# Depthwise convolution as fp32 products on 32x32 tiles of TensorE, pointwise product on 32x128 tiles

## The chip, the cores and the metric

The kernel runs on one core of a Trainium2 chip. The metric is the device time of one execution in microseconds; the profile's span, from the first to the last instruction, lies within a few tenths of a per cent of it. The core has five engines with queues of their own: TensorE (PE in the profile, its weight loads PEld), VectorE (DVE), ScalarE (ACT), GpSimd (POOL) and SyncE (SP), which issues DMAs. They work side by side and wait for each other through semaphores.

## What is computed

The input is 16 images of 128 channels and 28x28 points in fp32. A block of depthwise and pointwise convolution is added to it, then an attention over the 784 points of each image as tokens, then a mixture of eight experts. The change touches only the first block:

```python
h = conv(gn(x), dw_w, padding=1, feature_group_count=128)   # 3x3, one filter per channel
h = h + dw_b
h = relu(bn(h, bn1))
h = prune(h, 4.0)        # a channel whose maximum over the image is below 4.0 becomes zero
h = conv(h, pw_w)        # 1x1, 128 -> 128
h = h + pw_b
h = relu(bn(h, bn2))
h = prune(h, 0.001)
x = x + h
```

`gn` is a group norm over groups of four channels. After it come the spiking attention with a causal mask (queries, keys and values are projected and compared with thresholds) and the experts with their router.

## The kernel before

Each engine has its own instruction stream, written by hand, and the order in it is the order of the code. The image loop has 20 steps. Step k holds five stages at once, for different images: group norm of image k (`norm`), convolution of k-1 (`cnv`), transposes, layer norm and projections of k-2 (`add`), scores and attention of k-3 (`att`), the router and the sending of rows of k-4 (`moe`). Steps 0 to 5 and 14 to 19 are written out, the others run in a hardware loop, two steps a turn. After the loop come 105 tiles of 256 rows for the experts, and a last part that sums and writes the images.

The convolution of an image is a product per tap. Input and taps are split in two fp16 parts each: ScalarE writes the normalised image times 64 to `xn64` (L731) and its fp16 rounding to `padx[:, 0]` (L735), and GpSimd writes the rest to `padx[:, 1]` (L416). `make_taps` (L934, L937) puts the 9 taps of each channel on diagonals of 128x128, high and low part. `conv` (L475) then makes, for 9 taps and two halves of the image, three products (high-high, high-low, low-high) of 128x128 with 392 columns, 54 in all, which add up in PSUM `pair_a`. TensorE's `body` cuts these 54 into six pieces, `conv(..., first, end)` with 3 products to a unit: one unit after the scores 0 to 2, one after score 3, one after score 4, three after the transposes of `x1` and `t2`, eight after the attention, and four after the transposes of `xn`. Then come `queries`, `values`, `keys`, and last `pointwise`.

ScalarE's `first_relu` turns `pair_a` into `h1` (L742). VectorE's `mask_weights` takes the maximum of each channel (L1016), compares it with 4.0 (L1017) and scales the rows of the pointwise weights by the result (L1018, `pw_masked`). `pointwise` (L485) is two fp32 products of 392 columns. ScalarE's `second_relu` (L749) makes `h2`, and VectorE's `add_block` adds it to `x1`. On VectorE `mask_weights` stands between the spikes of the queries (`sq`) and those of the values (`sv`) and keys (`sk`), all L1032.

GpSimd does, in each step, the subtraction L416, the subtraction of the router's rows (L423) and 14 indirect DMAs (L428).

Engines' names for the four PSUM pairs of two banks are `pair_a` to `pair_d`; the convolution and the pointwise product both use `pair_a`.

## Time and profile before

| | us |
|---|---|
| median of 3 runs | 928.25 |
| lowest, highest | 926.79, 929.76 |
| profiled execution, its span | 927.2 |
| TensorE busy in it | 740.9 (80%) |
| VectorE busy | 687.4 (74%) |
| GpSimd busy | 525.4 (57%) |
| ScalarE busy | 480.0 (52%) |

The rows are read so: times are in us from the start of the span unless marked ns; `x` stands ahead of a number of records; L475 is a line of the kernel; in the names of tiles buffer numbers are left out, so that `h<-pair_a` is `h1` or `h2`, and `xn` in L731 is `xn64`. An fp32 product with a 128x128 stationary side shows as two records. A record of TensorE ends some time after the next one has started, since products are pipelined.

### The profile page before, as it was taken

Reading aid. Unit: us, or ns where it says so; the run is one execution under the profiler, and the core shown is the slowest. Engines: PE = TensorE matmul, PEld = TensorE weight load, DVE = VectorE, ACT = ScalarE, POOL = GpSimd, SP = SyncE. Lnnn points to the kernel's source line nnn. Section 1 sums busy time; section 2 is a strip of 40 time slices with the busy share of each in tenths; the row PEclk is TensorE's granted clock in tenths of the full one; section 3 lists DMA queues with packets and bytes.
Section 4 is the critical chain, followed back from the end, with each engine's and each line's share of the span. In section 5 each row is a group of like instructions: output and inputs, shape, how many; then the busy total and the mean of one; then the engine's idle time right before and its main releaser. Section 6 shows DMA issues by size and latency. Waiting matters only on the chain.

```text
span 927.2 us, 24122 instructions
## 1 busy us (share of the span) xinstructions
PE 740.9 (80%) x6865; PEld 578.0 (62%) x6866; DVE 687.4 (74%) x2275; ACT 480.0 (52%) x1102; POOL 525.4 (57%) x498
## 2 busy tenths in 40 slices
PE   1599989999999998996403999999999999994433
PEld 0255656666666665664302988889888988894322
DVE  2656887888888887865751898989888898884444
ACT  1235655566666664654302767777667766672000
POOL 4100176677777666665772576777677777765000
PEclk9989998999999998996555999999999999998555
DMA  7102132232323231221142232323222322222998
GB/s 151 58 18 76 53 111 89 83 106 81 105 83 107 79 107 42 66 71 48 61 85 53 68 89 72 86 82 83 80 80 76 85 84 83 75 79 54 269 286 234
DMA packets 76644, 85.72 MB, mean 92 GB/s; under 512 B 12491, under 2 KB 60655, under 8 KB 76610
## 3 DMA queue, kind: packets, MB, share of 16 engines
q1 hardware_dynamic: 59698, 52.85, 22.2%
q0 software_dynamic: 13888, 26.03, 8.9%
q10 hardware_dynamic: 3024, 6.43, 1.9%
q8 instruction: 17, 0.28, 0.1%
q14 instruction: 17, 0.14, 0.0%
HBM read 44.27 MB, written 35.48 MB: 86 GB/s over the span
## 4 chain that ended last, share of the span: by engine, by line
PE 65%; DVE 10%; DMA 8%; POOL 6%; issue 5%; ACT 4%; SPq 1%; POOLq 0%; DVEq 0%; ACTq 0%
PE pair_d L673 16%; PE pair_a L475 14%; PE pair_b L657 8%; PE pair_c L657 7%; DMA w<-expert_rows 6%; POOL dispatched_rows L428 4%; PE pair_c L506 3%; PE pair_a L645 3%; ACT seen_g L772 2%; PE pair_d L571 2%; PE pair_b L495 2%; PE pair_d L544 2%; PE pair_c L557 2%; PE pair_b L501 1%; DVE pw_masked L1018 1%
## 5 line engine op out<-in xcount | busy, mean ns | idle before, releaser
L438 POOL DMA_INDIRECT expert_rows<-xb_x,dest x210 | 243.0, 1157 | 114.3 <-issue 74.9
L428 POOL DMA_INDIRECT dispatched_rows<-rows,pos x224 | 217.5, 971 | 98.8 <-issue 63.8
L673 PE MATMUL pair_d<-w,xb_x 128*128 x2520 | 172.5, 220 | 0.0
L475 PE MATMUL pair_a<-padx,tap_diag 128*128 128x392 f16 x864 | 167.2, 341 | 0.9 <-ACT h L749 0.9
L673 PEld LDWEIGHTS pair_d<-w,xb_x 128*128 128x128 f16 x2520 | 153.0, 98 | 6.4
L1201 DVE TENSOR_TENSOR xb_x<-seen_g,xb_x 128x512 f16<-128x512 f32 x210 | 134.9, 681 | 0.0
L475 PEld LDWEIGHTS pair_a<-padx,tap_diag 128*128 128x128 f16 x864 | 84.5, 101 | 59.7 <-issue 6.0
L826 ACT ACTIVATE xrt<-pair_a 128x512 f16<-128x512 f16 x105 | 62.6, 597 | 113.4 <-PE pair_a L645 113.4
L1198 DVE CAST xb_x<-seen_g 128x512 f16<-128x512 f32 x210 | 89.9, 468 | 6.7 <-ACT seen_g L837 6.7
L837 ACT ACTIVATE seen_g<-pair_b,b 128x256 f32<-128x256 f32 x212 | 83.2, 475 | 6.2 <-PE pair_b L657 3.5
L837 ACT ACTIVATE seen_g<-pair_c,b 128x256 f32<-128x256 f32 x208 | 81.7, 475 | 5.4 <-PE pair_c L657 2.2
L657 PE MATMUL pair_b<-xrt,w 128*128 128x256 f16 x636 | 79.6, 276 | 1.8 <-ACT xrt L826 1.8
L657 PE MATMUL pair_c<-xrt,w 128*128 128x256 f16 x624 | 77.9, 275 | 1.9 <-ACT xrt L826 1.9
L645 PE MATMUL pair_a<-ident,xr 128*128 128x128 f16 x420 | 41.4, 223 | 45.0 <-DMA xr<-dispatched_rows 34.7
L416 POOL TENSOR_TENSOR padx<-xn,padx 128x784 f16<-128x784 f32 x16 | 26.2, 1637 | 89.9 <-ACT padx L735 89.7
L1187 DVE TENSOR_SCALAR small<-xr,tile_expert 128x2 f32<-128x2 f32 x105 | 27.6, 263 | 53.2 <-DMA expert_rows<-xb_x,dest 31.6
L657 PEld LDWEIGHTS pair_b<-xrt,w 128*128 x636 | 59.0, 98 | 11.6 <-issue 2.3
L657 PEld LDWEIGHTS pair_c<-xrt,w 128*128 x624 | 59.4, 99 | 8.5 <-issue 2.2
L789 ACT ACTIVATE root<-var 128x15 f32<-128x15 f32 x20 | 4.3, 214 | 107.1 <-DVE var L997 107.1
L645 PEld LDWEIGHTS pair_a<-ident,xr 128*128 128x128 f16 x420 | 27.6, 99 | 49.4 <-DMA xr<-dispatched_rows 34.8
L754 ACT ACTIVATE xn<-pair_b,shift,rstd 112x128 f32<-112x128 f32 x112 | 40.9, 466 | 20.6 <-DVE shift L1007 20.6
L506 PE MATMUL pair_c<-xt,w_t 128*128 128x272 f32 (+1 forms) x128 | 49.1, 507 | 1.1 <-ACT xt L762 1.1
(184 smaller groups left out, 1290.3 us busy)
## 6 DMA issues: line engine op xcount, KB each, us to landing
xr<-dispatched_rows SPq DMA_DIRECT2D x105, 131.0 KB
xb_x<-in_x SPq DMA_DIRECT2D x32, 392.0 KB, 3.8
w<-expert_rows SPq DMA_DIRECT2D x16, 784.0 KB, 7.1
t_all<-t SPq DMA_DIRECT2D x16, 392.0 KB
out<-w ACTq DMA_DIRECT2D x16, 392.0 KB, 6.4
w_stage<-in_L_ffn_W SPq DMA_DIRECT2D x16, 256.0 KB, 4.4
dispatched_rows<-rows,pos POOLq DMA_INDIRECT x224, 2.3
expert_rows<-xb_x,dest POOLq DMA_INDIRECT x210
```

The lines of the kernel that those rows point to most:

```text
L428: pool.indirect_dma_start(xs, bass.IndirectOffsetOnAxis(ap=pos[:, u, t, k:k + 1].bitcast(U32), axis=0), rows[:, u, t, :].bitcast(U32), Non ...
L438: pool.indirect_dma_start(ys, bass.IndirectOffsetOnAxis(ap=dest[:, u, s:s + 1].bitcast(U32), axis=0), y[:, u, s, :], None, bounds_check=ta ...
L475: last = T.matmul(pa[:, h * BANK:h * BANK + HALF], tap_diag[:, wp, tap, :], padx[:, xp, u, ky + 14 * h:ky + 14 * h + 14, kx:kx + SIDE], st ...
L506: last = T.matmul(pc[:, c0:c1], w_t[:, w, :], xt[:, c0:c1], start=True, stop=True)
L645: last = T.transpose(turned[:, c0:c0 + P], xr[:, u, s, part * P:(part + 1) * P], ident16[:])
L657: last = T.matmul(hp[:, f * TILE:(f + 1) * TILE], w1[:, wp, bass.ds(w0 + f * P, P)], xrt[:, u % 2, 2 * xp:2 * xp + 2, :].rearrange("p s k ...
L673: last = T.matmul(dst, ghl[:, u % 2, gp, f * TILE + s * P:f * TILE + (s + 1) * P], w2[:, wp, bass.ds(w0 + f * P, P)], start=False, stop=(f ...
L754: last = A.activation(out_[:, t, :], pair[0:TT, t * P:(t + 1) * P], ACT.Identity, scale=rstd[0:TT, n0 + t:n0 + t + 1], bias=shift[0:TT, n0 ...
L826: A.activation(xrt[:, u % 2, :, :].rearrange("p s k -> p (s k)"), turned[:, 2 * BANK * (u % 2):2 * BANK * (u % 2) + 4 * P], ACT.Copy).then ...
L837: A.activation(g[:, u % 2, f, :], hp[:, f * TILE:(f + 1) * TILE], ACT.Gelu, scale=1.0 / WSCALE, bias=b1[:, bass.ds(c0 + f, 1)]).then_inc(S ...
L1198: V.tensor_copy(ghl[:, u % 2, 0, h * 2 * TILE:(h + 1) * 2 * TILE], gv(u, h)).then_inc(S["g_hi_ready"], 1)
L1201: V.tensor_tensor(ghl[:, u % 2, 1, h * 2 * TILE:(h + 1) * 2 * TILE], gv(u, h), ghl[:, u % 2, 0, h * 2 * TILE:(h + 1) * 2 * TILE], ALU.subt ...
```

## The change

The input is no longer split. `padx` is fp32 and ScalarE writes it in one pass from `xb` (`xn64`, L731 and GpSimd's L416 are gone). The taps are no longer split either: `tap_diag` holds nine tables of 32 columns, made by one product in the set-up.

`conv` cuts the channels in four groups of 32 (`c`) and the image in four quarters of 7 rows (`q`). A product takes the 32 channels of `c` and writes the quarter `q` to the 32 partitions `q`, with 196 columns, on the 32x32 tile of rows `c` and columns `q`. A unit of the order in `body` is now one tap for two channel groups, eight products. The first nine units are the channel groups 0 and 1, the last nine 2 and 3; in between TensorE waits for its own products (`conv_half`), since groups 0 and 2, and 1 and 3, share a PSUM bank. The units stand where they stood. After it a partition holds channel 32c + r of quarter q at 32q + r.

So `first_relu` is four instructions, one for each channel group, with constants spread by TensorE in the set-up (`bn_q`). The maximum of a channel now lies in four partitions. `find_live` takes the maximum in each and compares it, `fold_live` adds the four comparisons up by a product on TensorE, and `mask_weights` compares the sum with 0.5 and scales a table of 128x512, the pointwise weights spread over the four quarters (`pw_q`). `pointwise` is 16 fp32 products of 196 columns on 32x128 tiles, in two halves with a wait of TensorE for itself in between. `gate` is a wait that stands as an instruction of its own.

```diff
-                for p in range(first, end):
-                    tap, h = p // 2, p % 2
+                for n in range(first, end):
+                    half, tap = n // TAPS, n % TAPS
+                    if n == TAPS:
+                        gate("conv_half", i + 1)
                     ky, kx = tap // 3, tap % 3
-                    for m, (wp, xp) in enumerate(((0, 0), (0, 1), (1, 0))):
-                        last = T.matmul(pa[:, h * BANK:h * BANK + HALF], tap_diag[:, wp, tap, :],
-                                        padx[:, xp, u, ky + 14 * h:ky + 14 * h + 14, kx:kx + SIDE],
-                                        start=(tap == 0 and m == 0), stop=(tap == TAPS - 1 and m == 2))
+                    for c in (2 * half, 2 * half + 1):
+                        for q in range(Q):
+                            last = T.matmul(pa[q * B:(q + 1) * B, quarter_at(c):quarter_at(c) + QL], tap_diag[c * B:(c + 1) * B, tap, :],
+                                            padx[c * B:(c + 1) * B, u, ky + QROWS * q:ky + QROWS * q + QROWS, kx:kx + SIDE],
+                                            start=(tap == 0), stop=(tap == TAPS - 1), tile_position=(c * B, q * B))
+                    if n == TAPS - 1:
+                        last.then_inc(S["conv_half"], 1)
                 if end == 2 * TAPS:
                     last.then_inc(S["conv_ready"], 1)
 
+            def fold_live(i):
+
+                pe.wait_ge(S["live_ready"], i + 1)
+                T.matmul(pa[:, QL:QL + Q], same[:, :, :].rearrange("p q b -> p (q b)"), live[:, 1, :], start=True, stop=True).then_inc(S["live_folded"], 1)
+
             def pointwise(i):
-                pe.wait_ge(S["pwm_ready"], i + 1)
-                pe.wait_ge(S["h1_ready"], i + 1)
-                for h in range(2):
-                    last = T.matmul(pa[:, h * BANK:h * BANK + HALF], pw_masked[:], h1[:, h * HALF:(h + 1) * HALF], start=True, stop=True)
+                gate("pwm_ready", i + 1)
+                for half in range(2):
+                    if half == 1:
+                        last.then_inc(S["pw_half"], 1)
+                        gate("pw_half", i + 1)
+                    for c in range(Q):
+                        for q in (2 * half, 2 * half + 1):
+                            last = T.matmul(pa[:, quarter_at(q):quarter_at(q) + QL], pw_masked[q * B:(q + 1) * B, c, :], h1[q * B:(q + 1) * B, c, :],
+                                            start=(c == 0), stop=(c == Q - 1), tile_position=(q * B, 0))
                 last.then_inc(S["pw_ready"], 1)
...
-                A.activation(xn64[:, :], xb[:, u, :], ACT.Identity, scale=gs[:, 22:23], bias=shift[:, GN:GN + 1]).then_inc(S["xn_ready"], 1)
                 if some(i - 1):
                     act.wait_ge(S["conv_ready"], i - 1)
-                act.wait_ge(S["xn_ready"], i + 1)
-                A.activation(padx[:, 0, u, 1:1 + SIDE, 1:1 + SIDE], xn64[:, :].rearrange("p (h w) -> p h w", w=SIDE),
-                             ACT.Identity).then_inc(S["xhi_ready"], 1)
+                A.activation(padx[:, u, 1:1 + SIDE, 1:1 + SIDE], xb[:, u, :].rearrange("p (h w) -> p h w", w=SIDE),
+                             ACT.Identity, scale=rstd[:, GN:GN + 1], bias=shift[:, GN:GN + 1]).then_inc(S["xn_ready"], 1)
...
-                A.activation(h1[:, :].rearrange("p (h c) -> p h c", h=2), halves(pa), ACT.Relu,
-                             scale=bn[:, 0, 2:3], bias=bn[:, 0, 7:8]).then_inc(S["h1_ready"], 1)
+                for c in range(Q):
+                    last = A.activation(h1[:, c, :], pa[:, quarter_at(c):quarter_at(c) + QL], ACT.Relu, scale=bn_q[:, 0, c:c + 1], bias=bn_q[:, 1, c:c + 1])
+                last.then_inc(S["h1_ready"], 1)
...
+            V.tensor_tensor(tap_diag[:, :, :], bc_mid(fold[:, :], TAPS), bc_last(dw_w[:, :], B), ALU.mult).then_inc(S["taps_ready"], 1)
...
-            def mask_weights(i):
+            def find_live(i):
 
                 link = Chain("dve_x", DVE_STEPS["x"] * i)
                 dve.wait_ge(S["h1_ready"], i + 1)
+                link(V.tensor_reduce(live[:, 0, :], h1[:, :, :], AX.X, ALU.max))
+                V.tensor_scalar(live[:, 1, :], live[:, 0, :], DW_THRESH, None, ALU.is_ge).then_inc(S["live_ready"], 1)
+
+            def mask_weights(i):
+
+                link = Chain("dve_x", DVE_STEPS["x"] * i + 1)
+                dve.wait_ge(S["live_folded"], i + 1)
                 if some(i):
                     dve.wait_ge(S["pw_ready"], i)
-                link(V.tensor_reduce(gs[:, 24:25], h1[:, :], AX.X, ALU.max))
-                link(V.tensor_scalar(gs[:, 25:26], gs[:, 24:25], DW_THRESH, None, ALU.is_ge))
-                V.tensor_scalar(pw_masked[:], w_t[:, 3, :], gs[:, 25:26], None, ALU.mult).then_inc(S["pwm_ready"], 1)
+                link(V.tensor_scalar(live[:, 2, :], pa[:, QL:QL + Q], 0.5, None, ALU.is_ge))
+                V.tensor_tensor(pw_masked[:, :, :], pw_q[:, :, :], bc_last(live[:, 2, :], P), ALU.mult).then_inc(S["pwm_ready"], 1)
```

On TensorE the end of a step, from the attention to the pointwise product, read before:

```order
L557 MATMUL pair_c<-seen_g,sv 128x112
L475 MATMUL pair_a<-padx,tap_diag 128x392 x24
L501 MATMUL pair_b<-ident,xn 128x112 [waits xn1_ready]
L501 MATMUL pair_b<-ident,xn 128x112 x6
L475 MATMUL pair_a<-padx,tap_diag 128x392 x12
L506 MATMUL pair_c<-xt,w_t 128x512 [waits xt_ready,gvar_ready,t2_ready]
L506 MATMUL pair_c<-xt,w_t 128x272
L525 MATMUL pair_b<-w_t,xt 112x128 x7
L506 MATMUL pair_c<-xt,w_t 128x512 [waits sq_ready]
L506 MATMUL pair_c<-xt,w_t 128x272
L485 MATMUL pair_a<-h,pw_masked 128x392 [waits h1_ready,pwm_ready]
L485 MATMUL pair_a<-h,pw_masked 128x392
```

and reads now:

```order
L497 MATMUL pair_a<-padx,tap_diag 32x196 x24
L497 MATMUL pair_a<-padx,tap_diag 32x196 [waits conv_half]
L497 MATMUL pair_a<-padx,tap_diag 32x196 x39
L535 MATMUL pair_b<-ident,xn 128x112 [waits xn1_ready]
L535 MATMUL pair_b<-ident,xn 128x112 x6
L497 MATMUL pair_a<-padx,tap_diag 32x196 x32
L540 MATMUL pair_c<-xt,w_t 128x512 [waits xt_ready,gvar_ready,t2_ready]
L540 MATMUL pair_c<-xt,w_t 128x272
L559 MATMUL pair_b<-w_t,xt 112x128 x7
L508 MATMUL pair_a<-live,same 128x4 [waits live_ready]
L540 MATMUL pair_c<-xt,w_t 128x512 [waits sq_ready]
L540 MATMUL pair_c<-xt,w_t 128x272
```

24 products have become 64 and 12 have become 32; the wait for `conv_half` falls into the piece after the attention, and the product with `live` and its wait stand between the values and the keys. Behind the keys now stand 8 products, a wait for `pw_half` and 8 more.

On VectorE the same end of a step read before:

```order
L1032 TENSOR_SCALAR sq<-pair_c 128x784 [waits q_ready,dve_z]
L1016 TENSOR_REDUCE gs<-h 128x1 [waits pw_ready,h1_ready]
L891 ISA
L1017 TENSOR_SCALAR gs<-gs 128x1 [waits dve_x]
L891 REGISTER_ALU
L1018 TENSOR_SCALAR pw_masked<-w_t,gs 128x128 [waits dve_x]
L1032 TENSOR_SCALAR sv<-pair_b 112x896 [waits v_ready]
L1032 TENSOR_SCALAR sk<-pair_c 128x784 [waits k_ready]
```

and reads now:

```order
L1067 TENSOR_SCALAR sq<-pair_c 128x784 [waits q_ready,dve_z]
L1043 TENSOR_REDUCE live<-h 128x4 [waits h1_ready]
L922 ISA
L1044 TENSOR_SCALAR live<-live 128x4 [waits dve_x]
L1067 TENSOR_SCALAR sv<-pair_b 112x896 [waits v_ready]
L1052 TENSOR_SCALAR live<-pair_a 128x4 [waits pw_ready,live_folded]
L922 REGISTER_ALU
L1053 TENSOR_TENSOR pw_masked<-pw_q,live 128x512 [waits dve_x]
L1067 TENSOR_SCALAR sk<-pair_c 128x784 [waits k_ready]
```

The making of `pw_masked` has moved behind `sv`, and has grown from 128 to 512 elements in each partition.

## Rows read from the trace of the kernel before

**Rows 1.** The page's busy times; then one step by engine (busy us, records, granted clock).

```profile
PE 740.9 (80%) x6865; PEld 578.0 (62%) x6866; DVE 687.4 (74%) x2275; ACT 480.0 (52%) x1102; POOL 525.4 (57%) x498
...
307.53:331.07 23.54, 22.41 (x147) 14.96 (x146) 19.96 (x77) 14.19 (x28) 17.29 (x17) 1.00 0.37 109
```

**Rows 2.** Timeline of that step, first part: start, length, engine, line, names, records.

```profile
312.59 0.26 ACT L772 ACTIVATE seen_g<-pair_d 112x112 bf16<-112x112 f32 x1
...
312.75 0.97 PE L495 MATMUL pair_b<-ident,xb_x 128*112 128x128 f32 x7 [0.28 <-ACT seen_g L772]
...
318.50 4.22 PE L475 MATMUL pair_a<-padx,tap_diag 128*128 128x392 f16 x24
...
319.93 2.56 ACT L754 ACTIVATE xn<-pair_b,shift,rstd 112x128 f32<-112x128 f32 x7 [1.28 <-DVE shift L1007]
...
322.56 0.87 PE L501 MATMUL pair_b<-ident,xn 112*128 112x112 f32 x7
```

**Rows 3.** Waits of TensorE: who waited for whom, total us, times, longest.

```profile
PE pair_a L485 <- DVE pw_masked L1018: 9.1, 3, 3.4
PE pair_b L501 <- ACT xn L754: 6.4, 2, 5.3
```

**Rows 4.** Timeline of that step, last part: TensorE, ScalarE, VectorE.

```profile
323.27 2.23 PE L475 MATMUL pair_a<-padx,tap_diag 128*128 128x392 f16 x12
...
325.33 1.48 PE L506 MATMUL pair_c<-xt,w_t 128*128 128x512 f32 x4
...
325.59 1.00 ACT L742 ACTIVATE h<-pair_a,bn 128x784 f32<-128x784 f32 x1 [0.51 <-PE pair_a L475]
...
326.65 1.69 PE L525 MATMUL pair_b<-w_t,xt 128*112 128x128 f32 x14
...
327.81 0.96 DVE L1016 TENSOR_REDUCE gs<-h 128x1 f32<-128x784 f32 x1
...
328.18 1.48 PE L506 MATMUL pair_c<-xt,w_t 128*128 128x512 f32 x4
...
328.81 0.15 DVE L1017 TENSOR_SCALAR gs<-gs 128x1 f32<-128x1 f32 x1
...
329.65 1.58 PE L485 MATMUL pair_a<-h,pw_masked 128*128 128x392 f32 x4
...
331.07 0.19 PE L579 MATMUL pair_d<-chosen,before 112*128 112x64 bf16 x1
```

**Rows 5.** Small products: timeline twice, then the group by line (busy us, mean ns).

```profile
314.33 1.45 PE L571 MATMUL pair_d<-wr_c,t 128*112 128x8 f32 x14
315.63 1.69 PE L475 MATMUL pair_a<-padx,tap_diag 128*128 128x392 f16 x9
...
331.10 0.32 PE L582 MATMUL pair_d<-chosen,ones 112*128 112x56 bf16 x7
...
L582 PE MATMUL pair_d<-chosen,ones 112*128 112x8 bf16 x16 | 2.7, 166 | 0.0
```

**Rows 6.** Timeline of the first step: the taps and the first convolution.

```profile
24.53 1.85 DVE L934 TENSOR_SCALAR tap_diag<-ident,dw 128x128 f16<-128x128 f32 x9
...
26.42 3.81 DVE L937 SCALAR_TENSOR_TENSOR tap_diag<-ident,dw,tap_diag 128x128 f16<-128x128 f32 x9
...
32.32 11.66 PE L475 MATMUL pair_a<-padx,tap_diag 128*128 128x392 f16 x54
```

**Rows 7.** Chain of work, its two longest L1018; then timelines of VectorE and GpSimd.

```profile
134.79 3.64 DVE pw_masked L1018
...
352.60 4.07 DVE pw_masked L1018
...
319.81 0.97 DVE L1046 TENSOR_TENSOR t<-pair_c,xb_x 128x784 f32<-128x784 f32 x1
...
353.15 1.64 POOL L416 TENSOR_TENSOR padx<-xn,padx 128x784 f16<-128x784 f32 x1
354.72 1.84 POOL L423 TENSOR_TENSOR rows<-xf,rows 112x896 f16<-112x896 f32 x1
```

96 lines of the change are left out of this document (56 added, 40 removed).

## The prediction, written before the changed kernel ran

> **What bounds the kernel now.** I read the page's table of engines first, then the stretches of one step of the image loop, then the waits of TensorE, then the timeline of that step. TensorE is busy 80% of the span, more than any other [rows 1]. The change touches the image loop only: the part up to about 430 us, in which 20 steps run and 16 of them hold a convolution. In the step from 307.53 to 331.07 TensorE is busy 22.41 of 23.54 us at the full granted clock (1.00), VectorE 19.96, GpSimd 17.29, ScalarE 14.19 [rows 1]. So at first sight every microsecond taken from TensorE's work is won. The timeline corrects that. The step holds four stretches, and in three of them TensorE's convolution pieces only fill a wait for someone else:
>
> - Scores: ScalarE's seven sign passes, of which the last starts at 312.59, set the pace, and the first transpose of the next piece starts at 312.75, released by them after a wait of 0.28 us [rows 2]. The first 9 of the 54 convolution records stand inside this.
> - From there to the transposes of `xn` at 322.56 runs a chain: the transposes at 312.75, statistics on VectorE (behind logits that don't depend on the convolution), scales, seven normalisations of 2.56 us from 319.93, which end at 322.49 [rows 2]. 33 convolution records stand in this stretch; they end just as the chain does. The waits view has TensorE waiting 6.4 us in two steps for this `xn` already [rows 3].
> - The last 12 records run from 323.27 to the projection at 325.33 [rows 4].
> - From 325.33 on TensorE alone decides: projections, then the pointwise product at 329.65, which was kept waiting by VectorE's `pw_masked` [rows 4].
>
> A faster convolution therefore finds the end of a chain in the first three stretches, and a slower tail costs in full.
>
> **The convolution itself.** Before: 54 records of 392 columns; 24 of them take from 318.50 to 322.56, 169 ns each, so 9.1 us per image [rows 2]. After: 144 products on 32x32 tiles with 196 columns, in fp32. An fp32 product is two records: two products of 512 and 272 columns show as x4, and take 325.33 to 326.65, which is 1.32 us for 2 x 784 columns, 0.84 ns a column and record [rows 4]. So 288 records of 196 x 0.84 = 165 ns each, 47.5 us if nothing overlaps. No row of this trace shows two tiles at work at once, so the cost is bounded from both sides. Low: eight tiles at a time, 16 records stream in 2 x 165 = 0.33 us, 18 such groups make 5.9 us. High: 47.5 us. Between them stand two floors that rows do show. Pairs of load and product with 8 to 56 columns start (0.32 - 0.17) / 6 = 25 ns apart [rows 5], which gives 288 x 25 = 7.2 us. With 8 columns and fp32 weights 14 records take from 314.33 to 315.63, 93 ns each for 112 weight columns, 0.83 ns a weight column [rows 5]; 32 columns are 27 ns and 288 loads 7.8 us. I take 7.8 us, because these two rows are the nearest to small tiles: one has many short products, the other small fp32 ones. The eight tiles of a group have places of their own in the array, and the two channel groups write to different banks, so nothing in the code orders them. To this comes one wait of TensorE for itself between the halves: a record of 8 columns lasts 0.166 us [rows 5], so the end of a product comes that long after its columns, and with a semaphore and a load I put it at 0.35 us. Sum 8.2 us in place of 9.1. The 0.9 us that this saves lie almost wholly in the first three stretches and are **costed at nothing**: the sign passes and the `xn` chain are late next. If that cover were gone they would be worth 16 x 0.9 = 14 us. In the third stretch 64 records of 27 ns take 1.7 us in place of 2.0, and ScalarE reaches the copy of `xt` one instruction sooner, since `padx` is written in one pass: **-0.3 us** a step.
>
> **The tail.** Three things grow here, all on the path.
> - ScalarE writes `h1` in four pieces. 128 columns take 2.56 / 7 = 0.37 us, 784 take 1.00 [rows 2, 4]; 196 columns come to 0.43, four to 1.7 in place of 1.0. `h1` is then ready at 325.59 + 1.7 = 327.3, and VectorE, busy with `sq` until then, takes it up at 327.81 [rows 4]: hidden by 0.5 us.
> - VectorE finds the live channels (reduction 0.96, comparison 0.15) by 328.96 [rows 4]. The new wait on TensorE stands behind `values` and ahead of `keys`. TensorE could have gone on at 328.18 and goes on at about 329.05; queued behind it are the keys, the pointwise product, the ranks and the next scores. The fold costs two loads, 0.2 us. VectorE then does `sv`, the second comparison (0.15) and the product of 128x512. 784 elements take 0.97 and 1 takes 0.15 [rows 4, 7], 1.05 ns each, so the 896 of `sv` take 1.08, until 329.98, and 512 take 0.69. That is 330.87, and the pointwise product starts at 330.95 in place of 329.65: **+1.3 us**.
> - The pointwise product is 16 products of 196 columns on 32x128 tiles, 32 records in place of 4, two row groups at a time: 32 x 165 / 2 = 2.6 us if two really stream together, 32 x 107 = 3.4 us if the loads of 128 fp32 weight columns (128 x 0.83) go one by one. I take 3.0, and 0.35 for the wait between its halves, in place of 1.42 (329.65 to 331.07) [rows 4]: **+1.9 us**.
>
> Net 1.3 + 1.9 - 0.3 = +2.9 us a step, x 16 = **+46.4 us**.
>
> **What goes for good.** In the first step the tap matrices take VectorE from 24.53 to 30.15, and the first convolution starts at 32.32 behind the statistics that come after them [rows 6]. The new table is one product of 128x288 in the set-up, where VectorE waits for ScalarE anyway; the longer set-up there (two reductions, three small products, five copies) is put at 2 us and lies ahead of the first scales, which wait for ScalarE, so it is costed at nothing; without that cover it costs its 2 us, once. The first convolution then starts near 26.7: **-5.6 us**. The subtraction L416 leaves GpSimd. Twice the 128x128 scaling L1018 took 3.64 and 4.07 us in place of 0.29 (L1016 and L1017 give 1.05 ns an element beside 0.15), and the second time it ends when GpSimd's L416 and L423 end, back to back (353.15 to 356.56) [rows 7]; TensorE waited for it 9.1 us in all, three times [rows 3]. With L416 gone only L423 is left to collide with, and I count 3.4 + 3.7 = **-7.1 us**. The Trainium skill (SBUF — State Buffer, SBUF: two separate sides) says that VectorE and GpSimd share a port pair; by it the new product, which reads two tables in SBUF, could still wait up to 1.8 us for L423, and 16 such waits would add 29 us, which I leave to the range.
>
> **Sum.** 46.4 - 5.6 - 7.1 = +33.7 us on the profiled 927.2 us; the median lies 1.05 us above the profiled span, so **962 us**. Ends of the forecast case, by step: tail +0.9, pointwise +1.5 and third stretch -0.9 give 1.5 x 16 - 12.7 = +11, 940 us; tail +1.6, pointwise +2.3, nothing in the third stretch and an allowance of 1 us for going in and out of the tiles, which no row shows, give 4.9 x 16 = +78, less 8 if GpSimd's L423 takes some of the gain back, = +70, 998 us.
>
> **Rivals.**
> 1. Records of one tile hold up the stream. The two records of one product stand next to each other on the same tile. If records start strictly in their order, the second waits until the first has streamed, and all behind it wait too; only the second record of one tile and the first of the next run together. Each product then costs 165 ns, 144 of them 23.8 us. For it: in every row of this trace starts follow the program. Against it: no row has two tiles. A step grows by 23.8 - 9.1 = 14.7, less 1.0 of TensorE's idle time that it fills (23.54 - 22.41), plus 3.2 in the tail: 16.9 x 16 - 12.7 = +258, **1186 us**. The Trainium skill (TensorE: Matmul & The Clock Gate, Part 3: Packing small matmuls — row/col tiling) says that products start and end strictly in program order; it also reports 10.6 times the speed for 16 tiles with one product each, which supports the forecast. No run here shows either yet.
> 2. No overlap at all: 47.5 us a convolution, 40.6 x 16 - 12.7: **1565 us**.
> 3. The granted clock falls. It is 1.00 in the step shown [rows 1]. If work on small tiles lets it drop to the lower level, 1.2 GHz, in the loop, the rest of TensorE's step, 22.41 - 9.1 - 1.4 = 11.9 us, doubles, the convolution becomes 18 x 0.66 = 11.8 and the pointwise product 5.6. With 1.3 of chain that is 42.4 us in place of 23.5: **1215 us**.
> 4. Not slower. The place is the `xn` chain and the tail: if what I call chains gives way because TensorE comes earlier to every step, and eight tiles stream fully, TensorE's own sum decides: 5.9 + 0.35 + 2.6 + 0.35 + 0.2 = 9.4 in place of 10.5, -1.1 x 16 - 12.7 = -30, **898 us**. It decides if the pointwise product starts less than 0.3 us later than before relative to the projections. The rows speak against it: `sq`, the reduction, `sv` and the mask stand on one engine in that order.
>
> **Chances.** Forecast case (940 to 998) 0.45; rival 1 0.30; rival 2 0.04; rival 3 0.05; rival 4 0.11; within 0.3% of before 0.05. A change under about 0.3% can't be told from none here. The range goes from 925 to 1215 and takes in the forecast case and rivals 1 and 3, 8 in 10. Faster 0.11, same 0.05, slower 0.84.
>
> **What would show it.** Records of the convolution: start to start about 27 ns in the forecast, 82 ns on average in rival 1, 165 in rival 2. In the forecast the convolution pieces between attention and the transposes of `xn` end early, and TensorE waits some tenths of a microsecond a step for ScalarE's `xn`; if no such wait appears, my cover is wrong. The pointwise product starts 5.6 us after the first projection in place of 4.3 and lasts 3.4. The granted clock stays 1.00. The first convolution starts near 26.7. The prediction is wrong if the records are not near 27 ns, or if the new wait for `live` costs nothing.

## The result, and the profile after

The changed kernel takes **1044.12 us** (median of four runs, 1028.8 to 1053.34) against 927.52 us of the kernel before beside it: a ratio of 1.115, 95% interval 1.106 to 1.124. A run more than 1.5% above the fastest of its kernel counts as slow, and every ratio here is that of the fast runs (of the changed kernel 1028.8 and 1042.71), while medians and ranges are those of all runs. The direction was as predicted and the time lies in the range of 925 to 1215, but the loss is 117 us between the medians and 107 by the ratio, where 34 were forecast. The profiled execution has a span of 1040.9 us, 113.7 more than before.

From the page of the changed kernel, the lines on the engines, on the granted clock in 40 slices, and on the two groups of tile products:

```profile
PE 828.8 (80%) x11099; PEld 653.9 (63%) x11100; DVE 676.6 (65%) x2266; ACT 478.9 (46%) x1134; POOL 496.7 (48%) x482
...
PEclk9998987686888787988875569999999999999555
...
L497 PE MATMUL pair_a<-padx,tap_diag 32*32 32x196 f32 x4608 | 144.9, 380 | 5.1 <-PE pair_a L497 4.1
...
L518 PE MATMUL pair_a<-h,pw_masked 32*128 32x196 f32 x512 | 58.3, 369 | 10.0 <-DVE pw_masked L1053 6.9
```

TensorE's share is 80% as it was [rows 1]. In the image loop, which fills the first half of the slices, the clock digits are 6 to 9. The digits 5 stand behind the loop.

Four stretches of the changed kernel: two whole steps, from one group mean to another, then two parts of the second. Columns: busy time and records of each engine, granted clock, share of DMA, GB/s.

```profile
104.36:130.81 26.45, 23.20 (x412) 16.76 (x411) 17.69 (x67) 15.16 (x33) 1.83 (x1) 1.00 0.15 48
324.60:358.38 33.78, 30.05 (x417) 20.77 (x414) 20.95 (x76) 14.34 (x31) 15.30 (x15) 0.77 0.25 76
336.77:345.86 9.09, 8.02 (x260) 5.84 (x259) 8.39 (x40) 4.53 (x10) 5.90 (x6) 1.00 0.43 135
345.86:361.49 15.63, 13.61 (x81) 9.27 (x73) 9.52 (x25) 7.58 (x15) 2.52 (x2) 0.72 0.21 58
```

The first step ran at the full clock and lasts 26.45 us, 2.91 more than the step of [rows 1]: the forecast said 2.9. The second has the same work and lasts 33.78 us at a mean of 0.77 of the full clock. Between 336.77 and 345.86 TensorE runs most of the convolution's tiles at 1.00, and behind them, from the projection on, the clock is lower (it was 0.58 too in the 12.17 us ahead of 336.77).

The timeline of TensorE in the step that stayed at the full clock, with two rows of ScalarE and VectorE (start, length, engine, line, names, records, idle time before and who ended it):

```profile
112.55 1.22 PE L497 MATMUL pair_a<-padx,tap_diag 32*32 32x196 f32 x48
...
116.59 1.89 PE L497 MATMUL pair_a<-padx,tap_diag 32*32 32x196 f32 x80 [0.22 <-PE pair_a L497]
119.33 0.89 PE L535 MATMUL pair_b<-ident,xn 112*128 112x112 f32 x7 [0.85 <-ACT xn L785]
120.15 1.56 PE L497 MATMUL pair_a<-padx,tap_diag 32*32 32x196 f32 x64
121.64 1.58 PE L540 MATMUL pair_c<-xt,w_t 128*128 128x512 f32 x4
...
121.88 1.74 ACT L773 ACTIVATE h<-pair_a,bn_q 128x196 f32<-128x196 f32 x4 [0.73 <-PE pair_a L497]
...
125.44 0.38 PE L508 MATMUL pair_a<-live,same 128*128 128x4 f32 x2 [0.69 <-DVE live L1044]
126.48 0.69 DVE L1053 TENSOR_TENSOR pw_masked<-pw_q,live 128x512 f32<-128x512 f32 x1
...
127.32 1.59 PE L518 MATMUL pair_a<-h,pw_masked 32*128 32x196 f32 x16
129.06 1.59 PE L518 MATMUL pair_a<-h,pw_masked 32*128 32x196 f32 x16
130.59 0.20 PE L613 MATMUL pair_d<-chosen,before 112*128 112x64 bf16 x1
```

48 tile records take 1.22 us and 64 from 120.15 to 121.64 take 1.49, so 23 to 25 ns each on average. A view of the convolution's records alone, in three short stretches behind 112.55, shows how they start (in brackets the records at work in the stretch):

```profile
112.50:112.60 0.10, 0.05 (x8) 1.00 0.00 0
112.60:112.73 0.13, 0.13 (x8) 1.00 0.00 0
112.73:112.80 0.07, 0.07 (x16) 1.00 0.00 0
```

Eight start within 0.05 us, then none until 0.19 us after the first, then eight more; in the trace the following eights are 0.165 us apart, the time of one record of 196 columns. So eight tiles do run side by side, and rivals 1 and 2 are out. TensorE now waits 0.85 us for `xn`. The pointwise product starts 127.32 - 121.64 = 5.68 us after the projection and lasts 3.27 us, 102 ns a record on average; in the trace its records start in pairs, 0.166 us from pair to pair, so two row groups stream together.

The same rows where the clock was low, from the step at 324.60:

```profile
345.86 2.93 PE L540 MATMUL pair_c<-xt,w_t 128*128 128x512 f32 x4
...
353.90 4.25 PE L518 MATMUL pair_a<-h,pw_masked 32*128 32x196 f32 x32 [1.09 <-DVE pw_masked L1053]
```

The projection takes 2.93 us in place of 1.58. TensorE's waits over the whole run (us, times, longest), to be read beside [rows 3]:

```profile
PE pair_b L535 <- ACT xn L785: 16.4, 14, 5.7
...
PE pair_a L508 <- DVE live L1044: 11.4, 16, 3.1
...
PE pair_a L518 <- DVE pw_masked L1053: 6.9, 6, 1.2
...
PE pair_a L497 <- PE pair_a L497: 4.1, 16, 0.4
```

The 9.1 us for `pw_masked` have become 6.9, the wait for `live` is new, 11.4 us, and the wait between the halves comes to 0.26 us each time.

Last the first steps of the loop. TensorE has stood idle, and then has nothing but the tile convolution of the first image for 12.5 us, with one wait of 0.22 us for itself between the halves:

```profile
26.36 6.13 PE L497 MATMUL pair_a<-padx,tap_diag 32*32 32x196 f32 x144
...
43.59 6.11 PE L518 MATMUL pair_a<-h,pw_masked 32*128 32x196 f32 x32 [1.07 <-DVE pw_masked L1053]
...
59.40 3.52 PE L497 MATMUL pair_a<-padx,tap_diag 32*32 32x196 f32 x80 [0.22 <-PE pair_a L497]
```

The first convolution starts at 26.36 (forecast 26.7), but a record takes 42.6 ns there, the pointwise product 6.11 us and 80 records 3.52 in place of 1.89. These are the lengths of the lower level. (The clock view has no mark that early and prints 1.00; the lengths of the same work are the evidence.) In the kernel before 54 full-array products stood in this place, 11.66 us [rows 6], 216 ns each beside 169 later on. By the starts in its trace the first 12 are some 320 ns apart and those from 37.7 us on 166: they began at the lower level and had the full one after about 5 us. Tile products did not bring the clock up in 12.5 us; the projections of the next step still take 2.72 us at 67.14, and the first records at the full level are those at 69.70.

**Where 113.7 us come from.** Steps at the full clock: 2.91 x 16 = 46.6. The start: 26.36 against 32.32, -6.0. The two stalls of L1018: -7.1. That leaves 113.7 - 46.6 + 6.0 + 7.1 = 80 us that the forecast does not have. Not all of them lie in the image loop. The first records of the experts' part behind it, which is the same in both kernels, start at 498.6 before and at 605.8 now (first and last start in us; shortest, median and longest in ns ahead of them):

```profile
L645 PE MATMUL pair_a<-ident,xr x420: 216/219/314, 498.6 to 836.1; 128*128 128x128 f16 x140
...
L682 PE MATMUL pair_a<-ident,xr x420: 216/219/314, 605.8 to 949.5; 128*128 128x128 f16 x140
```

So 107.2 us arose ahead of them and 6.5 behind, at a clock of 0.99 from their first to their last start in both kernels; the cause of the 6.5 stays open. Some 74 us of the loop are left, and the experiments are about these. An estimate from the clock views says that they can be the clock: 0.81 over the 340 us from 60 to 400 is 129 us at the lower level, 0.98 before is 14 (both views stand below), and 115 us more at half speed cost up to 58; to this come the first steps, at the lower level until 69.70, and the loop's part behind 400, which ends with the last projections at 538.1.

### The profile page after: what moved, and what is told of

The parts are those of the page before. It is cut to its first block, busy times and chain, and to the rows that moved or that the text cites. A ratio compares the mean times of both kernels' runs of the same rounds, so it can differ in the third digit from the quotient of the medians.

```text
span 1040.9 us, 32608 instructions
## 1 busy us (share of the span) xinstructions
PE 828.8 (80%) x11099; PEld 653.9 (63%) x11100; DVE 676.6 (65%) x2266; ACT 478.9 (46%) x1134; POOL 496.7 (48%) x482
## 4 chain that ended last, share of the span: by engine, by line
PE 62%; DVE 11%; DMA 7%; issue 6%; ACT 6%; POOL 5%; SPq 1%; POOLq 0%; DVEq 0%; ACTq 0%
PE pair_d L710 13%; PE pair_a L497 8%; PE pair_b L694 7%; PE pair_c L694 6%; PE pair_a L518 6%; DMA w<-expert_rows 6%; PE pair_c L540 5%; POOL dispatched_rows L436 4%; ACT xn L785 3%; PE pair_a L682 3%; PE pair_d L578 3%; PE pair_b L529 3%; PE pair_d L605 2%; DVE st L1013 2%; PE pair_d L603 2%
## 5 line engine op out<-in xcount | busy, mean ns | idle before, releaser
L446 POOL DMA_INDIRECT expert_rows<-xb_x,dest x210 | 238.6, 1136 | 124.9 <-issue 68.5
L436 POOL DMA_INDIRECT dispatched_rows<-rows,pos x224 | 220.6, 985 | 143.8 <-DVE pos L1128 76.3
L497 PE MATMUL pair_a<-padx,tap_diag 32*32 32x196 f32 x4608 | 144.9, 380 | 5.1 <-PE pair_a L497 4.1
L431 POOL TENSOR_TENSOR rows<-xf,rows 112x896 f16<-112x896 f32 x16 | 29.1, 1821 | 198.7 <-ACT rows L809 198.7
L497 PEld LDWEIGHTS pair_a<-padx,tap_diag 32*32 32x32 f32 x4608 | 85.3, 116 | 38.3 <-issue 25.5
L1234 DVE CAST xb_x<-seen_g 128x512 f16<-128x512 f32 x210 | 87.7, 458 | 6.4 <-ACT seen_g L868 6.4
L694 PEld LDWEIGHTS pair_b<-xrt,w 128*128 x636 | 59.3, 99 | 11.4 <-issue 2.2
L518 PE MATMUL pair_a<-h,pw_masked 32*128 32x196 f32 x512 | 58.3, 369 | 10.0 <-DVE pw_masked L1053 6.9
L540 PE MATMUL pair_c<-xt,w_t 128*128 128x272 f32 (+1 forms) x128 | 60.6, 604 | 1.1 <-ACT xt L793 1.1
L518 PEld LDWEIGHTS pair_a<-h,pw_masked 32*128 32x128 f32 x512 | 48.0, 205 | 20.6 <-issue 20.6
```

The source lines that it names most:

```text
L436: pool.indirect_dma_start(xs, bass.IndirectOffsetOnAxis(ap=pos[:, u, t, k:k + 1].bitcast(U32), axis=0), rows[:, u, t, :].bitcast(U32), Non ...
L446: pool.indirect_dma_start(ys, bass.IndirectOffsetOnAxis(ap=dest[:, u, s:s + 1].bitcast(U32), axis=0), y[:, u, s, :], None, bounds_check=ta ...
L497: last = T.matmul(pa[q * B:(q + 1) * B, quarter_at(c):quarter_at(c) + QL], tap_diag[c * B:(c + 1) * B, tap, :], padx[c * B:(c + 1) * B, u, ...
L518: last = T.matmul(pa[:, quarter_at(q):quarter_at(q) + QL], pw_masked[q * B:(q + 1) * B, c, :], h1[q * B:(q + 1) * B, c, :], start=(c == 0) ...
L540: last = T.matmul(pc[:, c0:c1], w_t[:, w, :], xt[:, c0:c1], start=True, stop=True)
L694: last = T.matmul(hp[:, f * TILE:(f + 1) * TILE], w1[:, wp, bass.ds(w0 + f * P, P)], xrt[:, u % 2, 2 * xp:2 * xp + 2, :].rearrange("p s k ...
```

## Experiments

Two theories stood against each other. **A**: TensorE's clock falls because convolution and pointwise product are now made of tile records. **B**: it falls because TensorE waits more (for `xn`, `live`, the mask) or has less to do. (In the expectations of the first three groups A is called T and B is called W.) Kernels in one group shared a chip and the runs of the kernel before.

### First group: each half of the change alone, on another chip

On this chip the kernel before takes 1145.8 us, 24% more than on the one of the prediction, so only ratios within the group are used.

`tile_conv_old_tail` is the changed kernel with the mask and the pointwise product made as before (`w_t` scaled by one comparison of the whole maximum, two full-array products). It leaves out the gathering of the quarters: each partition's maximum runs over what that partition holds, and the product sums over the partitions as they lie.

```diff
 def pointwise(i):
-    for c in range(Q):
-        for q in (2 * half, 2 * half + 1):
-            last = T.matmul(pa[:, quarter_at(q):quarter_at(q) + QL], pw_masked[q * B:(q + 1) * B, c, :], h1[q * B:(q + 1) * B, c, :], ..., tile_position=(q * B, 0))
+    for h in range(2):
+        last = T.matmul(pa[:, h * BANK:h * BANK + HALF], pw_masked[:, 0, :], h1[:, 2 * h:2 * h + 2, :].rearrange("p q l -> p (q l)"), start=True, stop=True)
...
-    fold_live(cnv[0])
```

> The convolution of the changed kernel (144 fp32 products on 32x32 tiles) with the tail of the kernel before (one first ReLU, mask of 128 elements ahead of sv, no fold, pointwise as two full-array products). The channels of h1 lie as the quarters left them, so that the pointwise product sums the wrong channels; the work is that of a full image. At a granted clock of 1.00 this should beat the kernel before: 927 - 5.6 (start) - 7 (L1018 behind L416) - 0.5 x 16 (last convolution piece) = about 907 us. Theory T (tiles): products on small tiles let the granted clock fall; then the clock is well under 0.90, near that of the changed kernel (0.845), and the time is 950 to 990 us. Theory W (waits): the clock falls because TensorE waits longer, for live, for the mask and for xn; this kernel has only the xn wait, so the clock is above 0.88 and the time 905 to 935 us.

`old_conv_new_tail` is the kernel before with the new tail alone: the 54 full-array products stay, `h1` is taken in four pieces, and `live`, the fold, the 128x512 mask and the 16 tile products follow as in the changed kernel. It leaves out the new layout: its partitions still hold whole channels, and the tail treats them as quarters.

```diff
+    fold_live(cnv[0])
...
 def pointwise(i):
-    for h in range(2):
-        last = T.matmul(pa[:, h * BANK:h * BANK + HALF], pw_masked[:], h1[:, h * HALF:(h + 1) * HALF], start=True, stop=True)
+    for half in range(2):
+        ...
+        for c in range(Q):
+            for q in (2 * half, 2 * half + 1):
+                last = T.matmul(pa[:, quarter_at(q):quarter_at(q) + QL], pw_masked[q * B:(q + 1) * B, c, :], h1[q * B:(q + 1) * B, c, :], ...)
```

> The convolution of the kernel before (54 fp16 full-array products, split input, L416 on GpSimd) with the tail of the changed kernel (four first ReLUs, fold on TensorE, mask of 512 elements behind sv, pointwise on 32x128 tiles). At the full clock the tail costs what one undisturbed step of the changed kernel shows, 1.5 us before the pointwise product and 1.95 in it: 927 + 16 x 3.45 - 7 = about 975 us. T: the convolution, two thirds of the tile records, is not on tiles here, so the clock stays above 0.88 and the time is 970 to 990. W: the waits for live and the mask are all here, so the clock falls nearly as in the changed kernel, and the time is 1010 or more.

`pw_full` is the changed kernel with only the 16 tile products of the pointwise part replaced by two full-array ones; fold, `live` and the 128x512 mask stay. The product reads one of the four weight tables, so it leaves the gathering of quarters out.

> The changed kernel with one edit: the pointwise product is two full-array products of 392 columns with one of the four weight tables, so that it takes a quarter of the weights and wrong channels; the rest, fold and mask included, is unchanged. Its own cost at the full clock: 3.27 - 1.32 = 1.95 us a step, 31 us. Both theories: 1044 - 31 = 1013 if the clock stays at 0.845. If the pointwise tiles are what lets the clock fall, the clock rises above 0.88 and the time is under 990.

`conv_third` is the kernel before with only the high-high products of the convolution, 18 in place of 54. It leaves out the low parts of input and taps.

```diff
-    for m, (wp, xp) in enumerate(((0, 0), (0, 1), (1, 0))):
+    for m, (wp, xp) in enumerate(((0, 0),)):
```

> The kernel before with one of its three fp16 products a tap and half (high parts only, 18 records an image in place of 54): the convolution at the precision of fp16. It measures what a shorter convolution is worth, and whether waits alone let the clock fall. 36 records less are 6.1 us of TensorE a step. If my reading of the two covered stretches holds, only the last piece counts (12 records become 4): -1.0 us a step, about 910 us. If TensorE's own sum decides, 830 us. T: the clock stays as in the kernel before (0.90). W: TensorE waits 4 to 5 us a step now, more than in the changed kernel, so the clock falls below 0.85 and eats the gain.

Measured: tile_conv_old_tail 1288 us (1267 to 1318; its two runs of 1267 and 1268 give a ratio of 1.107), old_conv_new_tail 1215 (ratio 1.059, 1.053 to 1.065), pw_full 1297 (1.128, 1.122 to 1.134), conv_third 1125 (0.979, 0.974 to 0.984). Waits of TensorE in tile_conv_old_tail, and then in conv_third:

```profile
PE pair_b L523 <- ACT seen_g L793: 100.2, 12, 12.4
PE pair_d L572 <- issue: 41.7, 10, 5.3
```

```profile
PE pair_b L501 <- issue: 80.0, 11, 10.9
```

Waits of 10 us for issue in the image loop belong to this chip; in [rows 3] TensorE waits for VectorE and ScalarE. What it teaches all the same: with TensorE standing that much, the tile convolution alone costs 11%, while the new tail alone costs 6%. All four were run again where the kernel before takes what it took.

### Second and third group: the same four, and three more

All on chips where the kernel before takes 926 to 927 us. The clock below is the view's mean over 60 to 400 us of the span.

> The changed kernel once more, unchanged, beside the others of this group, because the chip of the first group of experiments needed 1146 us for the kernel before. On a chip that needs about 928 for the kernel before, 1028 to 1053 is expected, clock 0.84 to 0.86.

> The same kernel as tile_conv_old_tail. On a chip that needs 928 us for the kernel before: theory T (tile products let the clock fall) 950 to 990 us and a clock under 0.90; theory W (waits do it) 905 to 935 and a clock above 0.88. The first chip gave +11% and a clock of 0.77, beside a kernel before that was 23% slow, which T alone had foreseen.

> The same kernel as old_conv_new_tail. On a chip that needs 928 us for the kernel before: T 970 to 990 with a clock above 0.88, W over 1010. If convolution and tail add up, this one's excess and that of tile_conv_old_tail_b together make the 113 us of the changed kernel; if the clock falls only when both are there, they make less.

> The changed kernel with TensorE kept at work where it waited: 16 full-array fp16 products with zero weights, 128 columns each, ahead of the wait for xn, and 36 bf16 products of 56 columns ahead of the wait for the mask, each about 0.9 us at the full clock, beside waits of about 0.9 and 1.1 us. They add nothing to the result. W: the clock rises to 0.88 or more and the time falls to 960 to 1000 us. T: the clock stays within 0.02 of the changed kernel's and the time is the same or up to 20 us longer.

`filled_waits` computes the same, with small products put into two waits of TensorE, for the mask and for `xn`; the wait for `live` is left as it was:

```diff
+    for _ in range(36):
+        T.matmul(pa[:, BANK + 200:BANK + 256], before[:], ones[:, 0:56], start=True, stop=True)
...
+        for _ in range(16):
+            T.matmul(pa[:, BANK + BANK // 2:BANK + BANK // 2 + P], b2[:, 0:P], ident16[:], start=False, stop=False)
```

> old_conv_new_tail_b with two of the three fp16 products a tap and half (the low part of the taps is left out): 36 full-array records, 36 x 169 = 6.1 us, beside 7.3 us of 288 tile records in the changed kernel. So TensorE waits for xn, for live and for the mask as long as in the changed kernel or longer, and only the kind of the convolution's records differs. Theory T (tile records let the clock fall): the steps stay near 27 us with hardly any time at the lower clock between 60 and 400 us (under 20), total 980 to 1000 us. Theory W (waits): 80 us or more at the lower clock there and over 1020 us.

`two_thirds_new_tail` is `old_conv_new_tail` with two of the three products a tap and half, so that TensorE has less full-array work and more to wait. It leaves out the products with the low part of the taps.

> The same kernel as pw_full: the changed kernel with two full-array products for the pointwise step (a quarter of the weights, wrong channels). At the full clock 1.95 us a step less than the changed kernel's 26.45. T, with convolution tiles alone to blame: the time at the lower clock between 60 and 400 us stays near that of the changed kernel (89 and 129), total about 1010. If pointwise tiles and convolution tiles must both be there: it falls to the 34 of tile_conv_old_tail_b, total 950 to 970.

> The same kernel as conv_third: the kernel before with 18 of 54 full-array records (high parts only). T: no time at the lower clock beyond the 14 us of the kernel before, and steps of 22.5 in place of 23.5 us, since only the last piece lies outside the chains: about 910 us. W: TensorE idles 5 us a step, so the clock falls as in the changed kernel, steps are 25 us or longer and the time is over 940.

| kernel | median us | ratio (95%) | clock, 60 to 400 |
|---|---|---|---|
| the changed kernel again (after_again) | 1044.3 | | 0.87 |
| tile_conv_old_tail_b | 933.1 | 1.005 (1.001 to 1.009) | 0.95 |
| old_conv_new_tail_b | 995.7 | 1.076 (1.070 to 1.082) | 0.99 |
| filled_waits | 1047.3 | 1.131 (1.124 to 1.138) | 0.84 |
| two_thirds_new_tail | 998.3 | 1.076 (1.070 to 1.082) | 0.93 |
| pw_full_b | 954.7 | 1.031 (1.026 to 1.036) | 0.95 |
| conv_third_b | 945.1 | 1.019 (1.015 to 1.024) | 0.87 |

The changed kernel itself has 0.81, 0.87 and 0.77 from 60 to 400 us in its three profiles (the first, after_again and after_beside), so a difference of a few hundredths between two kernels says nothing.

**The convolution alone** costs 6 us, where the gains at the start and at L1018 had promised -12.7. The time lies in B's range (905 to 935), not in A's (950 to 990). Two steps of tile_conv_old_tail_b:

```profile
145.00:168.37 23.37, 21.08 (x380) 14.79 (x380) 18.50 (x74) 14.48 (x30) 15.06 (x16) 1.00 0.29 89
168.37:193.17 24.80, 22.57 (x380) 16.30 (x380) 19.57 (x76) 13.45 (x28) 15.99 (x16) 0.93 0.35 106
```

At the full clock a step lasts 23.37 us, as before [rows 1], with 1.3 us less of TensorE's work: the cover is what the prediction took it for. In its waits view

```profile
PE pair_b L529 <- ACT xn L775: 17.0, 15, 5.3
```

is the wait for `xn`, 15 times for 16 images. The other kind of step has a stretch of lower clock and is 1.4 us longer.

**The tail alone** costs 68.7 us, and a step of it (old_conv_new_tail_b) never leaves the full clock:

```profile
159.30:186.40 27.10, 24.79 (x185) 17.12 (x181) 19.02 (x75) 16.00 (x34) 16.65 (x16) 1.00 0.25 77
```

That is 3.6 us a step more, where the prediction's two terms of the tail give 1.3 + 1.9 = 3.2. The total of 995.7 misses both ranges, A's 970 to 990 and B's 1010 or more. The two halves come to 6.1 + 68.7 = 75 us apart and to 117 together by the medians, or 99 by the one run of after_again that enters a ratio (1025.64): 24 to 42 us arise only where both stand in one kernel.

**Which part of the tail.** In pw_full_b 32 tile records become four full-array ones, in fp32 as before, and the wait between the halves goes with them. The time falls from 1044 to 955, into the range (950 to 970) expected if the loss needs both kinds of tiles. Two steps of it:

```profile
174.60:199.45 24.85, 21.64 (x390) 15.11 (x386) 20.06 (x76) 14.18 (x30) 15.93 (x16) 1.00 0.36 105
199.45:225.90 26.45, 23.13 (x389) 16.46 (x386) 19.02 (x74) 15.21 (x32) 15.15 (x16) 0.94 0.25 77
```

At the full clock the step is 26.45 - 24.85 = 1.6 us shorter than that of the changed kernel, 26 us over 16 steps. The other 64 of the 90 us (45 of 71, if the run of 1025.64 is taken) go with the clock, 0.95 in place of 0.77 to 0.87. A expects that. B can point to the wait between the halves, which is gone too.

**B's own evidence.** conv_third_b has no tile product and yet is slower than the kernel before, by 1.9%, with a third of the convolution. A step of it, and its longest wait:

```profile
212.50:239.20 26.70, 19.65 (x109) 12.23 (x110) 22.17 (x76) 13.89 (x28) 17.98 (x16) 0.90 0.32 96
```

```profile
PE pair_b L501 <- ACT xn L754: 57.5, 16, 4.1
```

TensorE is busy for 19.65 of 26.70 us and the clock is 0.90. So standing still goes with a lower clock too, and with 36 of 54 products taken away the kernel became slower: B had said over 940, A 910. (On the chip of the first group the same kernel was faster than the one before, ratio 0.979.) The clock is not the whole of it. This step also holds a wait of 2.44 us for `pw_masked`, and over the run the waits for it come to 18.9 us (11 times) in place of 9.1 [rows 3]. But filled_waits stayed at 0.84 and 1047 us, as A had said (B: 960 to 1000). Its filling worked where it was put: the wait for `xn` is left once, 4.4 us, in place of 14 times, 16.4 us, and none for the mask is left. The wait for `live` was not filled and is still there (13.3 us). two_thirds_new_tail, with two thirds of the full-array convolution, took 2.6 us more than old_conv_new_tail_b. Its time is the one that A gave (980 to 1000), but its clock of 0.93, 48 us at the lower level, is neither A's under 20 nor B's 80. After these runs neither theory stood alone, since every kernel with more tile work in the convolution also had less full-array work.

### Fourth group: the same time added, in tiles or in full-array products

The changed kernel ran beside two that add some 7 us to its steps. `conv_tiles_twice` makes each half of the tile convolution twice; the second pass starts the sum again, so the result is the same.

```diff
-    for n in range(first, end):
-        half, tap = n // TAPS, n % TAPS
-        if n == TAPS:
+    for n in range(2 * first, 2 * end):
+        half, tap = n // (2 * TAPS), n % TAPS
+        if n == 2 * TAPS:
```

`conv_tiles_and_full` adds 42 full-array bf16 products on the data of the image, whose sums are thrown away:

```diff
+ def full_array(u, n):
+     for k in range(n):
+         T.matmul(pc[:, BANK:BANK + HALF], w_t[:, 3, :].bitcast(BF16)[:, 1::2],
+                  padx[:, u, k:k + 14, 1:1 + SIDE].bitcast(BF16)[:, :, 1::2], start=True, stop=True)
```

with 7 behind each of the first three units of the convolution, and 21 behind the next three. They stand only in the steps that hold an attention as well as a convolution: 588 records in the profile, 14 steps. The doubled tiles stand in all 16.

> The changed kernel once more, to stand on the same chip beside the next two. Both theories: 1026 to 1056 us as measured before, with 89 to 129 us at the lower clock between 60 and 400 us of the profile.

> The changed kernel with each half of the tile convolution made twice (the second pass starts the sum again, so that the result is the same): 288 more tile records a step, 7.0 us at 24.5 ns each. At the full clock a step of 26.4 us becomes about 30 (some 3 us of it fill waits that TensorE has now), 1040 us in all. Theory A (tile records count for little with the clock, what counts is full-array streaming): the stretches at the lower clock, 89 to 129 us between 60 and 400 us in the changed kernel, stay or grow, and the kernel takes 1100 to 1180. Theory B (what counts is how long TensorE stands or waits, whatever it runs): low stretches shrink below 60 us, and the kernel takes 1040 to 1070.

> The changed kernel with 42 full-array bf16 products of 392 columns (upper halves of the fp32 image and of the pointwise weights) added to each step between the scores and the attention, their sums thrown away: 42 x 165 ns = 6.9 us, as much as the tile convolution a second time in the run beside it. Both theories expect the lower clock's stretches below 60 us between 60 and 400 us, and 1040 to 1070. If the low stretches stay near 100 us here too (1100 or more), neither full-array streaming nor busy time in the first half of the step is what the clock wants, and what is left is the second half: the waits and short products from the transposes of xn to the rank.

Measured: the changed kernel 1065 us (1022 to 1069), conv_tiles_twice **1288** (1270 to 1291, ratio 1.380), conv_tiles_and_full **1107** (1094 to 1114, ratio 1.198). Over the whole execution the granted clock is 0.748 to 0.770 in the four runs of conv_tiles_twice, 0.888 to 0.906 in those of conv_tiles_and_full, 0.817 to 0.861 in those of the changed kernel beside them, and 0.901 to 0.908 in those of the kernel before. The loop from 60 to 400 us, by kernel. Before:

```profile
60.00:400.00 340.00, 316.46 (x2013) 210.04 (x2013) 271.57 (x986) 199.05 (x392) 204.20 (x191) 0.98 0.28 84
```

The changed kernel, in the profile shown above:

```profile
60.00:400.00 340.00, 305.00 (x4330) 209.58 (x4314) 202.71 (x738) 153.43 (x321) 130.14 (x126) 0.81 0.21 65
```

conv_tiles_twice:

```profile
60.00:400.00 340.00, 316.24 (x5242) 216.40 (x5246) 142.20 (x520) 101.03 (x212) 75.44 (x75) 0.72 0.15 47
```

conv_tiles_and_full:

```profile
60.00:400.00 340.00, 308.51 (x4294) 201.43 (x4278) 180.19 (x664) 136.53 (x287) 112.43 (x112) 0.96 0.19 60
```

**This tells the theories apart.** conv_tiles_twice took longer than even A's range of 1100 to 1180. It keeps TensorE busy for 316.24 of 340 us, to within a quarter of a microsecond what the kernel before has, and its clock is 0.72 against 0.98. Its waits for `xn` are down to one, and the clock fell further all the same. With the same time a step in full-array products the clock is 0.96. B fails as the whole account: busy time as such does not keep the clock up, and seven microseconds of tiles do not do what seven of full-array products do. Two things differ beside the tiles. The added full-array products are bf16 and the tiles fp32; in pw_full_b, where both sides were fp32, the clock rose as well. And the full-array products all stand ahead of the attention, while the doubled tiles are spread over the step; that was not tried apart. In conv_tiles_twice one stretch shows tiles at the lower level directly, first by the clock, then in the timeline:

```profile
347.17:353.96 6.79, 6.79 (x161) 4.83 (x162) 0.74 (x6) 0.00 (x0) 0.00 (x0) 0.50 0.26 87
```

```profile
347.17 6.79 PE L497 MATMUL pair_a<-padx,tap_diag 32*32 32x196 f32 x160 [0.22 <-PE pair_a L497]
```

160 records in 6.79 us are 42.4 ns each, as good as the 42.6 of the first convolution above, and 6.8 us of nothing but tiles did not lift the clock from 0.50.

I had put conv_tiles_and_full at 1040 to 1070 us; it took 1107. The clock did as expected, the hiding did not. A step of it at the full clock:

```profile
142.10:175.70 33.60, 31.01 (x461) 20.76 (x457) 20.13 (x76) 14.22 (x31) 15.16 (x15) 1.00 0.25 78
```

It is 33.60 - 26.45 = 7.15 us longer, all that was added. The products stand ahead of the attention, where the kernel before had 18, and push the end of the scores and the chain behind it. Over 14 steps that is 100 us; the kernel lost only 42 by the medians against the changed one beside it (1065), so some 58 us came back, with the clock. The figure is rough, since the runs of the changed kernel go from 1022 to 1069: against its fastest only 16 us came back. conv_tiles_twice lost 223 against the same median, of which its own work at the full clock is at most 7.1 x 16 = 113.

### A version that beats both

`mask_and_taps` keeps the split convolution and goes after the two things that the change gained: it puts `make_taps` ahead of the first scales, and, where the change had taken L416 off GpSimd, it moves the making of `pw_masked` from VectorE to ScalarE. It computes everything.

```diff
+ def mask_weights(i):                      # on ScalarE
+     act.wait_ge(S["dve_x"], DVE_STEPS["x"] * i + 2)
+     A.activation(pw_masked[:], w_t[:, 3, :], ACT.Copy, scale=gs[:, 25:26]).then_inc(S["pwm_ready"], 1)
...
-     V.tensor_scalar(pw_masked[:], w_t[:, 3, :], gs[:, 25:26], None, ALU.mult).then_inc(S["pwm_ready"], 1)
```

> The kernel before with two moves and the whole computation: pw_masked is made by ScalarE, between the normalisation of xf and rows, in place of VectorE's L1018; and the tap tables are made ahead of the first scales, where VectorE waits 4.8 us for ScalarE (18.4 to 23.2), in place of behind them. L1018's two long waits behind GpSimd's L416 and L423 (3.4 and 3.8 us) and five short ones of 0.3 go, and 4.8 us at the start: 927 - 7 - 1 - 4.8 = about 914 us, if my reading of L1018 and of the start holds; no change if the stall moves to another instruction of VectorE and the first step waits for something else.

Measured: **916.3 us** (910.2 to 919.4), ratio 0.988 (0.983 to 0.992) to the kernel before; about 914 had been expected. The gain is small, 1.2%, but the interval leaves out 1. Its step, its first group mean, and TensorE's pointwise group (busy, mean ns, idle before and who ended it):

```profile
156.80:180.20 23.40, 22.15 (x153) 14.98 (x149) 19.61 (x75) 14.44 (x30) 17.81 (x17) 1.00 0.38 111
```

```profile
26.23 0.59 PE L461 MATMUL pair_c<-gs,group_avg 128*128 128x2 f32 x2 [9.39 <-DVE gs L975]
28.49 11.64 PE L475 MATMUL pair_a<-padx,tap_diag 128*128 128x392 f16 x54 [1.67 <-POOL padx L416]
```

```profile
L485 PE MATMUL pair_a<-h,pw_masked 128*128 128x392 f32 x64 | 25.2, 518 | 2.7 <-ACT pw_masked L747 2.7
```

The first convolution starts 3.8 us earlier than in [rows 6], and the waits for the mask come to 2.7 us in place of the 9.1 of [rows 3].

## Why the prediction was right in direction and wrong in size

**The failed step is the granted clock.** The forecast case had it at 1.00 throughout, and rival 3, in which it falls, had a chance of 0.05 and was priced as if the whole loop ran at the lower level (1215 us). What happened is between: the forecast case's own changes and, on top, a clock of 0.77 to 0.87 in the loop. About 74 of the 113.7 us are left for it by subtraction; no run measures this share directly, and 6.5 more lie behind the loop and stay unexplained. The error had two parts. The prediction looked at the one row it had, a clock of 1.00 in a step [rows 1], and took it for a property of the loop; it depends on what TensorE runs in the loop. And it treated the falling clock as a case by itself in place of an addition to each of the others.

The Trainium skill (TensorE: Matmul & The Clock Gate, Part 1: The HAM clock gate) says that the gate follows how busy TensorE has been. Here busy time of 316.46 and 316.24 us in 340 went with 0.98 and 0.72, so busy time as the profile counts it does not decide alone; the measurement decides. The Trainium skill (TensorE: Matmul & The Clock Gate, Part 4: PE-mode transpose) says of transposes that they don't count as busy in the same way; no run here tried that for transposes.

Step by step:

- **Convolution, 288 records at 27 ns, 7.8 us**: the size was near, by luck. It took 23 to 25 ns a record at the full clock, 6.6 to 7.3 us in all. Neither of the two floors that gave 7.8 sets this: the records start in eights, a few ns apart, and each eight waits for the one before to stream, 0.165 us. That is the mechanism of the low bound of 5.9 us (36 x 0.165). The price of 42.5 ns at the lower level was not in it.
- **The wait between the halves, 0.35**: 4.1 / 16 = 0.26.
- **Gain hidden under the sign passes and the `xn` chain**: right, as the 0.85 us before L535 and tile_conv_old_tail_b (a step of 23.37) show.
- **The tail, +1.3 and +1.9**: right. The pointwise product starts 5.68 us after the projection (5.6 forecast) and lasts 3.27 (3.35 forecast). The middle value of 3.0 was between two mechanisms, and the records show the lower one: two row groups stream together (2.6), and the rest is two starts and two ends. In old_conv_new_tail_b the two cost 3.6 and not 3.2.
- **Start, -5.6**: -6.0, but TensorE stayed at the lower level until 69.70, and so gave part of that back.
- **Stalls of L1018, -7.1**: gone, but the -7.1 was read too high. 3.4 and 3.7 are what VectorE took longer; of TensorE's three waits the longest is 3.4 [rows 3], and the two that go with these stalls are 3.0 and 3.4 in the trace. And the mask of 128x512 has its own. The view of that one line (shortest, median and longest in ns):

```profile
L1053 DVE TENSOR_TENSOR pw_masked<-pw_q,live x16: 691/693/1833, 42.7 to 507.7; 128x512 f32<-128x512 f32 x16
```

and its group among the lines (busy us, mean ns, idle before):

```profile
L1053 DVE TENSOR_TENSOR pw_masked<-pw_q,live 128x512 f32<-128x512 f32 x16 | 16.5, 1031 | 0.6
```

The median is the forecast 0.69 us, and the longest as long as GpSimd's L431 (1.83 us in this kernel). Five of the 16 take 1.71 to 1.83 us; each of them starts while L431 is at work, and ends behind it. The 16 take 16.5 us in all, 5.4 more than 16 x 0.69. The prediction's rule from the Trainium skill (SBUF — State Buffer, SBUF: two separate sides), that the product of two tables would wait for GpSimd, agrees with the trace where they meet; they met in five steps, and it cost at most 5.4 us, not 29.

- **Rivals 1 and 2**: out, by 24 ns a record. The order of starts that rival 1 rests on does hold in the records, but eight of them start within 0.05 us, so it holds up nothing; the sentence of the Trainium skill cited there (TensorE: Matmul & The Clock Gate, Part 3: Packing small matmuls — row/col tiling) is not contradicted.
- **Rival 3**: the nearest to what happened. It named the cause and gave it 0.05; its own terms add up to 1218, not 1215.
- **Rival 4**: the tail's order was as the rows said; out.
